# Attention chunks: every 64x64 product in four corners, state terms ahead of the inverses, gate sums on TensorE

## The reference

```
kn = k / max(|k|, 1e-12);  pred = S^T kn;  r = clip(v - pred, -1, 1)
S = a * S;   S += beta  * kn (v - S^T kn)^T        (a, aR: sigmoid gates per key channel)
R = aR * R;  R += gamma * kn (r - R^T kn)^T
o = S^T q + R^T q
```

## Time and profile before

| what | us |
| --- | --- |
| median of 3 runs | 3306.05 (3304.01 to 3314.07) |
| the profiled execution | 3276.76, of which the span of the profile is 3274.9 |
| busy: PE, DVE, ACT, POOL | 2773.5, 2721.3, 1943.8, 953.5 |

### The profile page before, as it was taken

The page is one execution under the profiler, slowest core; times in us unless marked ns, Lnnn a source line. Parts: engine busy times, 40 slices in busy tenths (PEclk is TensorE's granted clock), DMA queues, the critical chain, the costliest instruction groups (busy, mean ns, idle before and its releaser), DMA issues. The chain is left out here.

```text
span 3274.9 us, 132532 instructions
## 1 busy us (share of the span) xinstructions
PE 2773.5 (85%) x55642; PEld 2460.6 (75%) x55642; DVE 2721.3 (83%) x6827; ACT 1943.8 (59%) x5180; POOL 953.5 (29%) x928
## 2 busy tenths in 40 slices
PE   3888888888888888888888888888886199999986
PEld 3878888887787888788788888888786177777664
DVE  2889898888989988999999999999997156777776
ACT  2656555556666655666666555666654077666664
POOL 3112222222222222223222222233221101444444
PEclk8988898888888988989999899999998599999998
DMA  3321111111111111111111111111110945777776
GB/s 116 82 64 37 36 35 35 35 35 37 39 35 35 37 37 35 43 35 35 39 40 41 35 35 35 35 42 35 39 40 30 347 144 170 221 217 224 220 217 180
DMA packets 209563, 264.55 MB, mean 81 GB/s; under 512 B 30673, under 2 KB 183250, under 8 KB 208210
## 3 DMA queue, kind: packets, MB, share of 16 engines
q1 hardware_dynamic: 183936, 188.53, 19.0%
q0 software_dynamic: 24576, 67.27, 7.2%
q10 hardware_dynamic: 466, 0.27, 0.0%
HBM read 125.37 MB, written 130.58 MB: 78 GB/s over the span
## 5 line engine op out<-in xcount | busy, mean ns | idle before, releaser
L379 POOL DMA_INDIRECT table<-tail,places x256 | 277.1, 1082 | 721.1 <-DVE BR L852 214.8
L1496 PE MATMUL bank<-w,tail 128*128 x1280 | 357.2, 401 | 31.4 <-ACT tail L1539 14.5
L1468 POOL DMA_INDIRECT tail<-y_table,places x256 | 249.5, 975 | 449.3 <-DMA y_table<-tail 314.0
L1091 POOL COPY inv_r<-N 32x512 f32<-32x512 f32 x128 | 136.4, 1065 | 734.0 <-DVE N L827 730.0
L445 DVE TENSOR_TENSOR tri<-tri,step 128x58 f32<-128x58 f32 (+13 forms) x896 | 305.5, 341 | 30.8
L444 DVE TENSOR_TENSOR step<-tri 128x58 f32<-128x58 f32 (+13 forms) x896 | 301.4, 336 | 26.4
L1496 PEld LDWEIGHTS bank<-w,tail 128*128 128x128 f32 x1280 | 219.2, 191 | 95.9 <-issue 72.7
L1586 DVE TENSOR_TENSOR more<-tail 128x1 f32<-128x1 f32 x320 | 50.8, 159 | 193.7 <-ACT tail L1548 189.6
L1511 PE MATMUL bank<-w,tail 128*128 x640 | 191.1, 380 | 2.7 <-DVE tail L1597 1.4
L1546 ACT ACTIVATE tail<-bank 128x129 f32<-128x129 f32 x320 | 89.8, 281 | 158.9 <-PE bank L1496 156.3
L1482 PE MATMUL bank<-ident,tail 128*128 128x128 f32 x640 | 125.1, 278 | 66.1 <-DMA tail<-table 65.6
(11 more groups left out here) (275 smaller groups left out, 8103.8 us busy)
## 6 DMA issues: line engine op xcount, KB each, us to landing
table<-blank SPq DMA_DIRECT2D x320, 128.5 KB, 3.2
tail<-table SPq DMA_DIRECT2D x320, 128.5 KB
y_table<-tail SPq DMA_DIRECT2D x320, 128.0 KB
w<-in_wpack_dram SPq DMA_DIRECT2D x16, 1540.0 KB, 19.3
tail<-in_x_dram SPq DMA_DIRECT2D x66, 64.0 KB, 2.5
x_rows<-tail SPq DMA_DIRECT2D x32, 128.0 KB
sh_rows<-tail SPq DMA_DIRECT2D x32, 128.0 KB, 1.9
table<-tail,places POOLq DMA_INDIRECT x256, 2.9
```

The source lines that it names most:

```text
L379: nc.gpsimd.indirect_dma_start(out=table, out_offset=bass.IndirectOffsetOnAxis(ap=t.places[:, TOP * (n - 1) + k:TOP * (n - 1) + k + 1], ax ...
L1468: nc.gpsimd.indirect_dma_start(out=t.term[2 * (m % 2) + k], out_offset=None, in_=d.y_table[0:P * closed(b) + P + 1, :], in_offset=bass.Ind ...
L1496: mm = nc.tensor.matmul(ps[:, 0:257], t.xT_slot[i % 3][:, P * kt:P * kt + P], weights(i, 257 * kt, 257), start=(kt == 0), stop=(kt == 1))
```

## The change

1. Gates: gate_projection makes a0, a1, r0 and r1 with tokens in partitions (the input is the stationary operand, 512 features stream), three products over 512 columns per bank, the third being a one-row product of ones and the bias. exp_gate becomes one exponential of 512 columns per bank. running_sums multiplies by a triangle of ones (t.running), eight products of 128 columns per gate, and gives sums with features in partitions as before, in new WIDE jobs C00 to C11 behind q; the scans leave VectorE (in the attention loop; the first chunk's own front keeps them), and decays reads the banks, right behind the copies of q, ahead of the shared expert's sigmoid.
2. Corners: PQ, RQ, KT, SU and RU go by four corners too. The units are dealt to banks by odd, pair, mixed and out_unit, and the tensors pqT, rqT, kT, U, B and V are stored in matching orders (at_pair, at_mixed, at_out).
3. Order: the terms of O and PR that need only the states are made ahead of SG, in two pieces each, the first with corners flipped, with a wait between the pieces; O and PR hold their banks until "free". X1 goes behind PR, SU comes behind X1; the addition to S goes ahead of the keys' scaling; the copy of XT goes ahead of the first root on ScalarE.
4. Two more constants are loaded at the start (running, 128x128, and gate_row, 128x512).

```diff
-    jobs += two("Z") + two("X") + two("PR") + two("U") + two("SU") + two("NS") * front + two("O") + [("SD", "")]
-    jobs += two("W") + two("RU") + ends + [("RK", "")] * route + [("OUT", "")] + two("V") * front
+    jobs += [("KT", f"{g}{h}") for g in range(2) for h in range(2)] + two("q") * front + [("C", f"{g}{i}") for g in range(2) for i in range(2)] * front + [("SG", "")]
+    jobs += two("O") + two("PR") + two("Z") + [("X", "0")] + two("U") + free("PR") + [("X", "1")] + two("SU")
+    jobs += two("NS") * front + [("SD", "")]
+    jobs += two("W") + free("O") + two("RU") + ends + [("RK", "")] * route + [("OUT", "")] + two("V") * front
     return jobs
...
+def odd(i, s):
+    return 2 * i + s
...
+def pair(i, s):
+    return 4 * (i // 2) + 2 * s + i % 2
...
+def mixed(i, s):
+    return 2 * i + (s ^ i % 2)
...
+def out_unit(i, s):
+    b1 = i // 2 % 2
+    return 8 * (i // 4) + 4 * (s ^ b1) + 2 * b1 + i % 2
...
+            def four(banks, unit, pairs, first=True, last=True, whole=False, rows=range(8), flip=0):
+                for i in rows:
...
                         if whole:
-                            begin, end = first and i == 0 and begin, last and i == 7 and end
+                            begin, end = first and i == rows[0] and begin, last and i == rows[-1] and end
                         for s in range(2):
                             u = unit(i, s)
                             for j in range(2):
-                                r, to = slice(C * j, C * j + C), slice(C * (j ^ s), C * (j ^ s) + C)
+                                r, to = slice(C * j, C * j + C), slice(C * (j ^ s ^ flip), C * (j ^ s ^ flip) + C)
...
+            def gate_projection(n, name, w, g):
+                for i in range(2):
+                    ps = begin(n, f"{name}{i}")
+                    for kt in range(2):
+                        nc.tensor.matmul(ps[:, :], t.xnT[:, kt, :], w[:, kt, 512 * i:512 * i + 512], start=(kt == 0), stop=False)
+                    at = 32 * (2 * g + i)
+                    nc.tensor.matmul(ps[:, :], t.ones_sq[at:at + 1, :], t.gate_row[at:at + 1, :], start=False,
+                                     stop=True, tile_position=(at, 0)).then_inc(t.sem["front_mm"], 1)
+            def running_sums(n, g):
+                pe.wait_ge(t.sem["log_ready"], 2 * n + g + 1)
+                for i in range(2):
+                    ps = begin(n, f"C{g}{i}")
+                    for m in range(4):
+                        mm = nc.tensor.matmul(ps[:, P * m:P * m + P], t.z[:, g, 512 * i + P * m:512 * i + P * m + P],
+                                              t.running[:, :], start=True, stop=True)
+                    mm.then_inc(t.sem["front_mm"], 1)
...
                 mm.then_inc(t.sem["front_mm"], 1)
                 need(pe, t, "queries_made", o.base("queries_made", n))
-                for i in range(4):
-                    ps = begin(n, f"PQ{i}")
+                for e in range(2):
+                    banks = [begin(n, f"PQ{2 * e + h}") for h in range(2)]
                     for m in range(4):
-                        u = 4 * i + m
-                        for j in range(2):
-                            r = slice(C * j, C * j + C)
-                            mm = nc.tensor.matmul(ps[r, 2 * C * m:2 * C * m + 2 * C], t.kminus[0][r, u, :],
...
+                        for h in range(2):
+                            u = pair(4 * e + m, h)
+                            for j in range(2):
+                                r, to = slice(C * j, C * j + C), slice(C * (j ^ h), C * (j ^ h) + C)
+                                mm = nc.tensor.matmul(banks[h][to, 2 * C * m:2 * C * m + 2 * C], t.kminus[0][r, u, :],
+                                                      t.pq[r, :, u, :], start=True, stop=True)
...
+                                mm.then_inc(t.sem["mm_done"], 1)
                 if front:
                     for i in range(2):
...
-                    units(n, f"RQ{h}", h, [(of(t.kminus[1]), of(t.rqplus))])
+                crossed(n, "RQ", pair, [(of(t.kminus[1]), of(t.rqplus))])
                 for g in range(2):
-                    for h in range(2):
-                        units(n, f"KT{g}{h}", h, [(of(t.kminus[g]), lambda r, u: t.eye[r, :])])
...
                         projection(n, f"q{i}", t.wq, i)
+                if front:
+                    running_sums(n, 0)
+                O, PR = both(n, "O"), both(n, "PR")
+                queries = [(of(t.S), lambda r, u: t.pq[r, 1, u, :]), (of(t.R), of(t.rqplus))]
+                keys = [(lambda r, u: t.pq[r, 0, u, :], of(t.S))]
+                four(O, out_unit, queries, last=False, whole=True, rows=(2, 3, 6, 7), flip=1)[1].then_inc(t.sem["O_flipped"], 1)
+                four(PR, mixed, keys, last=False, whole=True, rows=(1, 3, 5, 7), flip=1)[1].then_inc(t.sem["PR_flipped"], 1)
+                pe.wait_ge(t.sem["O_flipped"], n + 1)
+                four(O, out_unit, queries, first=False, last=False, whole=True, rows=(0, 1, 4, 5))
+                pe.wait_ge(t.sem["PR_flipped"], n + 1)
+                four(PR, mixed, keys, first=False, last=False, whole=True, rows=(0, 2, 4, 6))[1].then_inc(t.sem["O_begun"], 1)
...
+                    running_sums(n, 1)
                 ps = begin(n, "SG")
...
+                def second_product(g):
+                    wait_emptied(pe, t, o, n, f"Z{g}")
+                    ps = begin(n, f"X{g}")
+                    for u in range(16):
+                        for j in range(2):
+                            top = slice(C * j, C * j + Q)
+                            mm = nc.tensor.matmul(ps[top, Q * u:Q * u + Q], t.T[top, 16 * g + u, :],
+                                                  t.Z[top, 16 * g + u, :], start=True, stop=True)
+                    mm.then_inc(t.sem["mm_done"], 1)
                 pe.wait_ge(t.sem["N_ready"], n + 1)
                 for g in range(2):
...
-                for g in range(2):
...
-                    mm.then_inc(t.sem["mm_done"], 1)
-                PR = [begin(n, "PR0"), begin(n, "PR1")]
-                four(PR, odd_unit, [(lambda r, u: t.pq[r, 0, u, :], of(t.S))], last=False, whole=True)
+                second_product(0)
...
-                crossed(n, "U", [(of(t.inv[0]), of(t.B))])
+                crossed(n, "U", mixed, [(of(t.inv[0]), of(t.B))])
                 wait_emptied(pe, t, o, n, "U1")
-                for ins in four(PR, odd_unit, [(lambda r, u: t.pqT[r, u, 0, :], of(t.U))], first=False, whole=True):
+                for ins in four(PR, mixed, [(of_pq(0), of(t.U, at_mixed))], first=False, whole=True):
                     ins.then_inc(t.sem["PR_done"], 1)
-                for h in range(2):
-                    units(n, f"SU{h}", h, [(of(t.kT[0]), of(t.U))])
...
                 if front:
                     pe.wait_ge(t.sem["keys_squared"], n + 1)
                     for i in range(2):
...
-                ins[1].then_inc(t.sem["O_begun"], 1)
+                four(O, out_unit, [(of(t.U, at_mixed), of_pq(1))], first=False, last=False, whole=True)
                 ps = begin(n, "SD")
                 wait_emptied(pe, t, o, n, "SG")
...
-                    units(n, f"RU{h}", h, [(of(t.kT[1]), of(t.B))])
+                crossed(n, "RU", pair, [(of(t.kT[1], at_pair), of(t.B, at_mixed))])
                 if front:
                     triangles(n)
...
-                dve.wait_ge(t.sem["log_ready"], 2 * n + gate + 1)
-                nc.vector.tensor_tensor_scan(t.c[:, gate, :, :].rearrange("p u n -> p (u n)"), t.restart[:],
-                                             t.z[:, gate, :], 0.0, ALU.mult, ALU.add).then_inc(t.sem["scan_done"], 1)
...
-                    wait_done(dve, t, o, n, "KT11")
-                    running_sum(n, 0)
-                    running_sum(n, 1)
                 dve.wait_ge(t.sem["sh_sig_ready"], n + 1)
...
+                    nc.vector.tensor_tensor(by_pair(t.S, h), in_pairs(ps), by_pair(t.S, h),
+                                            ALU.add).then_inc(t.sem["dve_emptied"], 1)
                 if front:
                     keys = t.k[:].rearrange("p u n -> p (u n)")
                     dve.wait_ge(t.sem["norm_ready"], n + 1)
                     link(nc.vector.tensor_tensor(keys, keys, t.tri[:].rearrange("p c i -> p (c i)"), ALU.mult))
...
-                for h in range(2):
-                    ps = mm(n, f"SU{h}")
-                    nc.vector.tensor_tensor(t.S[:, half[h], :], blk(ps[:, :]), t.S[:, half[h], :],
-                                            ALU.add).then_inc(t.sem["dve_emptied"], 1)
                 if front:
...
-                    for m in range(4):
-                        hp = 4 * i + m
-                        ins = nc.scalar.activation(t.z[:, gate, P * hp:P * hp + P], ps[:, P * m:P * m + P], ACT.Exp,
-                                                   bias=t.neg_bias[:, gate, hp:hp + 1], scale=-1.0)
-                    ins.then_inc(t.sem["front_act"], 1)
```

(17 more changed lines are left out.)

161 lines of the change are left out of this document (82 added, 79 removed).

## The result

| | kernel before | changed kernel |
| --- | --- | --- |
| median, range, runs (us) | 3305.0, 3296.1 to 3314.1, 4 | 3510.8, 3504.5 to 3511.6, 4 |
| ratio to before, 95% interval | | 1.0618 [1.0587, 1.065] |
| profiled execution, its span (us) | 3276.8, 3274.9 | 3504.5, 3502.6 |

What follows compares the result with a forecast made beforehand. VectorE and TensorE passing turns bound the chunk at 77.0 us; TensorE's queue would take over: 20.6 + 10.6 + 16.9 + 30.3 = 78.4 us, +47 us in all with loading and semaphores, 3353 us; range 3265 to 3446.

Steps and rivals of the forecast that it cites:

- the ring: Chain of last-ending waits that sets a chunk's period; TensorE's queue was to take it over, 3.1 us above VectorE's.
- the queue from r to Z: TensorE's work from the first product of r to the first Z product; forecast at 30.3 us per chunk.
- stretch 1: From the first Z product to the keys' scaling on VectorE; forecast 20.6 us, bounds 18.0 and 21.9.
- Stretch 2 and r: Keys' scaling to first mask on VectorE, 10.6 us; then first mask to first product of r, 16.9 us.
- The queue's sum: TensorE, r to Z: 23.55 us up to SG, plus and minus edited products, one wait and SG itself, 30.3 us.
- One-row products: Gate bias products in r on TensorE; upper end taken, 0.46 us each over 512 columns, r +1.7 us.
- TensorE stays in time: Rival: TensorE from r to Z under 27.2 us, so VectorE rules; faster, 3197 us; chance 0.18.
- The two effects cancel: Rival: cheap bias products in r, about 3310 us, or upper clock kept after Z, 3269 us; chance 0.20.
- The lower clock spreads: Rival: NS and product a slowed by half clock, +3 us per chunk, 3446 us; chance 0.12.

Runs made afterwards that it cites:

- e2: Changed kernel without the one-row bias products of the gate projections (gate biases left out); chunk shorter by 1.4 us.
- e3: Changed kernel with PR's state term moved behind the second pair of running sums, ahead of SG; chunk shorter by 1.0 us.
- e4: Changed kernel with PR's state term moved behind X0, where TensorE waits for the inverses; chunk shorter by 2.0 us.
- e11: Changed kernel with its four running sums spread between the q projections and state terms; chunk shorter by 1.4 us.
- e1: Changed kernel with the gate half undone, corners and order kept; 0.9964 times the kernel before.
- e6: Kernel before with the corners alone, gates and order of before; 0.9954 times the kernel before.
- e9: Changed kernel with 19 unread products of 128 columns in TensorE's waits behind Z, X0 and U; 1.0401 times the kernel before.
- e12: Changed kernel with running sums spread, PR's state term behind X0 and 13 unread products in TensorE's waits; 1.0163 times the kernel before.
- e5: Kernel before with the gate half alone changed, running sums between q and SG; 1.099 times the kernel before.

## Why the prediction was wrong

The mechanism was right: TensorE's queue took over the ring. The size was not: two terms of the sum were too small, the queue from r to Z by 3.3 us per chunk and stretch 1 by 1.7.

- **The ring**: right. From r to Z TensorE's queue replaces VectorE's 42 us as what ends last, Z follows SG, SG waits (1.17 us, forecast 1.2), L902 stands idle over 4 us, L920 still waits for the norms. VectorE's share fell by 9 points, not 6. e2, e3, e4 and e11 show the ring by shortening it.
- **Stretch 2 and r**: right, 10.45 and 16.86 us against 10.6 and 16.9. The order does this: corners alone have keys to masks at 11.8, with the order it is 10.4. But e1 against e6 shows no gain in the whole chunk, since Z to the keys took the 1.4 us back.
- **The queue's sum, 30.3 us**: this step failed, by 3.3. Averages over chunks 3 to 28: r 5.9 instead of 5.5 (an instruction over 512 columns takes 0.48 us on the mean with 128 rows and 0.53 with one, not 0.46). The running sums 4.1 instead of 3.7 and SG 1.98 instead of 1.84. The state terms 3.9 instead of 3.0: the spacing was nearly right (0.017, forecast 0.016), but there are pauses such as the 0.91 us in the rows above, for which the profile names no releaser. PQ and KT together 4.8 instead of 3.9, with 0.4 of such pauses in KT and PQ in part at 1.2 GHz. These are 0.4 + 0.5 + 0.9 + 0.9 = 2.7; the remaining 0.6 is spread over the other groups. Two causes run across them: 1.3 us of unreleased pauses per chunk (2.45 idle less the 1.17 ahead of SG), and 1.3 us per chunk at 1.2 GHz, which cost about 0.6 (PQ and the k products are that much shorter in e4, which has none). The sum took every row at its best spacing and allowed for neither.
- **Stretch 1, 20.6 us**: this step failed too, by 1.7. Its place and its reason were right (U 7.55 us behind Z, forecast 7.4; TensorE waits and the clock falls), but I weighed the fast end, 18.0, in as one third. The low clock comes in every one of the 26 chunks, and the stretch is at the slow end, 22.3 against 21.9. The forecast had NS back at the upper clock; the low clock lasted to 18.3 us behind Z on the mean, and NS took 2.9 us and ended at 19.3, not 18.8. Even with the clock up (e9) it is 19.0, not 18.0.
- **One-row products**: the upper end was right. They stand 0.53 us apart, no less than products over 128 rows. The Trainium skill's rule in the prediction holds here. They fill 2.1 us of r to Z; leaving them out (e2) gained 1.5, the clock taking back the rest.
- **Rivals**: "TensorE stays in time" needed a queue under 27.2 us; even e12, without its waits, has 29.2 of work in its window. "The two effects cancel" needed cheap one-row products or a clock that stays up; neither came. "The lower clock spreads" was closest with 3446, but r was not late; the clock took its toll in Z to the keys, NS included, and in the queue itself.
- Together: 1.7 + 3.3 - 0.15 = 4.9 us per chunk missed, of the 83.3 - 78.4 measured.

Not settled: what the pauses in the state terms and KT wait for, which of the waits behind Z (or the small products between them) brings the clock down, and why some chunks have the low clock between r and Z, where TensorE hardly waits.

## What to carry to other kernels

When a change moves work onto an engine whose queue has only a microsecond of room, add up that queue with mean rows (pauses and lower clock in them), not with its best spacings: many groups, each a few tenths of a microsecond long, were the larger error here. Put operand-ready work into waits that exist anyway (PR's term cost nothing behind X0; in the queue it took 1.4 of the 2.0 us that e4 gained), and give products whose banks another engine must empty a neighbour of another kind. A change of three parts is three changes: here two of them, with one term moved, make the kernel 1.5% faster (0.9854, interval 0.9826 to 0.9883), and the third costs 6.6 to 9.9%: 1.0618 against 0.9964 with the other two, 1.099 by itself.

## What the runs showed of the hardware

- No wait behind Z was longer than 2.44 us (1.7, 2.1 and 1.15 on the mean, with 1.2 to 2 us of products between them), and yet TensorE ran at 1.2 GHz for 13.7 us or more in every chunk. The fall came 3.2 to 5.6 us behind the first Z product, before the second of these waits was over. With all three filled with products to pauses of 0.44 us at most, the clock stayed at 2.4 GHz from Z to the keys in 25 chunks of 26.
- Filling waits did not make the clock's low time vanish: in r to Z, without any new wait, it rose from 1.3 to 2.9 us per chunk (e9), and was 5.3 in e5, the kernel with the longest r to Z.
- Too much filling delays the next product: a filler takes 0.24 us, and 28 of them put U 2.4 us later.
- A product over 512 columns from one row took no less than one from 128 rows: 0.53 against 0.48 us per instruction.
